# Turning and projecting finished attention tiles inside the last two groups, and a new order of the first context loads

## The reference

```python
q = query @ Wq.T + bq;  k = key @ Wk.T + bk;  v = value @ Wv.T + bv
attn = softmax(q @ k.T)          # layer 0: scaled, masked, then a product with Wo
out = attn @ v
x = x + out
```

## Time and profile before

| what | value |
|---|---|
| median of 3 runs | 1501.59 us (1499.8 to 1501.68) |
| the profiled execution | 1503.77 us, its span 1502.0 us |
| PE busy | 1430.5 us, 95% of the span |
| DVE, ACT, POOL busy | 64%, 50%, 22% |
| mean granted clock of PE | 0.987 of full speed |
| stage 0 with its start; stages 3 and 6 | about 0 to 151 us; 363 to 491 us; 585 to 715 us |

### The profile page before, as it was taken

How to read it: one execution, slowest core, us unless ns; L and a number is a source line. 1 busy time by engine, 2 the same in 40 slices (tenths; PEclk the granted TensorE clock), 3 DMA queues, 4 the chain that set the end, 5 groups by cost and what they waited for, 6 DMA issues and landing times.

```text
span 1502.0 us, 26221 instructions
## 1 busy us (share of the span) xinstructions
PE 1430.5 (95%) x10513; PEld 979.6 (65%) x10513; DVE 967.1 (64%) x1667; ACT 750.2 (50%) x1379; POOL 331.2 (22%) x439
## 2 busy tenths in 40 slices
PE   7899999999999999999999989999989899999998
PEld 4797666887888655898565545555545454555697
DVE  4776645544787534787363378889989892567533
ACT  5574342113665424664442337777777676325232
POOL 3784340002643213642103041110000000100000
PEclk9999999999999999999999999999999999999999
DMA  9314132221212410211315365545757412310140
GB/s 373 129 57 181 63 121 92 95 85 36 73 69 107 151 59 35 91 57 55 106 70 186 51 173 92 85 76 87 177 79 146 93 20 106 161 57 2 57 169 14
DMA packets 43008, 147.74 MB, mean 98 GB/s; under 512 B 6380, under 2 KB 21996, under 8 KB 34028
## 3 DMA queue, kind: packets, MB, share of 16 engines
q1 hardware_dynamic: 42888, 146.07, 33.7%
HBM read 123.49 MB, written 22.56 MB: 97 GB/s over the span
## 4 chain that ended last, share of the span: by engine, by line
PE 83%; DVE 9%; ACT 4%; issue 2%; POOL 2%; DMA 0%; SPq 0%; ACTq 0%; POOLq 0%; DVEq 0%
PE PS L163 51%; PE PS L2399 8%; PE PS L2311 7%; PE PS L2296 5%; PE PS L634 2%; PE PS L1660 2%; DVE SM L2415 2%; PE PS L1889 1%; POOL CNr L932 1%; PE PS L1910 1%; PE PS L2390 1%; PE PS L2985 1%; PE PS L1917 1%; PE PS L2890 1%; DVE SM L306 1%
## 5 line engine op out<-in xcount | busy, mean ns | idle before, releaser
L2415 DVE TENSOR_REDUCE SM<-PS 128x1 f32<-128x1024 f32 x256 | 301.8, 1219 | 42.4 <-PE PS L2296 41.1
L163 PE MATMUL PS<-ARr 128*128 128x256 f32 (+1 forms) x672 | 177.2, 323 | 0.8 <-POOL CNr L932 0.8
L2311 PE MATMUL PS<-AR 49*128 49x256 bf16 (+1 forms) x1216 | 162.9, 271 | 1.1 <-DVE AR L2436 0.7
L163 PE MATMUL PS<-HT,AR 128*128 128x512 f32 x328 | 153.4, 616 | 2.6 <-ACT HT L355 1.1
L163 PE MATMUL PS<-CNr,ARr 128*128 128x256 f32 x672 | 130.7, 292 | 11.6 <-DVE ARr L801 10.7
L2311 PE MATMUL PS<-AR,CT 49*128 49x256 bf16 (+1 forms) x832 | 124.6, 272 | 0.0
L163 PE MATMUL PS<-ARr,HTr 128*128 128x512 f32 x384 | 122.3, 400 | 0.5 <-issue 0.5
L163 PEld LDWEIGHTS PS<-ARr 128*128 128x128 f32 x672 | 114.9, 190 | 10.1 <-issue 1.2
L862 ACT CAST ARr<-PS 128x512 fp32r<-128x512 f32 x96 | 56.3, 586 | 112.5 <-PE PS L634 112.5
L163 PEld LDWEIGHTS PS<-HT,AR 128*128 128x128 f32 x328 | 61.4, 195 | 78.0 <-issue 74.1
L163 PE MATMUL PS<-AR 128*128 128x256 f32 (+3 forms) x504 | 109.5, 371 | 1.4 <-DVE AR L720 0.8
(11 more groups left out here) (403 smaller groups left out, 2727.7 us busy)
## 6 DMA issues: line engine op xcount, KB each, us to landing
CN<-ctx_n SPq DMA_DIRECT2D x24, 1024.0 KB, 5.6
AR<-k_parts SPq DMA_DIRECT2D x114, 128.0 KB
k_parts<-CN SPq DMA_DIRECT2D x32, 384.0 KB, 3.3
CT<-pack SPq DMA_DIRECT2D x6, 2048.0 KB, 7.6
AR<-pack SPq DMA_DIRECT2D x20, 512.0 KB, 4.6
CT<-k_parts SPq DMA_DIRECT2D x78, 128.0 KB
CT<-ctx_t SPq DMA_DIRECT2D x8, 1024.0 KB, 19.1
v_ones<-CN SPq DMA_DIRECT2D x28, 288.0 KB, 3.0
```

Of the source, the lines that this page charges most:

```text
L163: last = te.matmul(o, l, r, start=first and k == 0, stop=final and k == n - 1, skip_group_check=True)
L2311: return te.matmul(PS[:, b, z * 256:z * 256 + 256], keys[rows, c * 128:c * 128 + 128], QQ9[rows, pr, rest, cols], start=not rest, stop=boo ...
L2415: ve.tensor_reduce(MX9[:, p % 2, e, g % 8 // 4, g % 4:g % 4 + 1], PS[:, b:b + 2, :].rearrange("p a b -> p (a b)"), AX, ALU.max).then_inc(* ...
```

## The change

In stages 3 and 6 the first two tiles are turned and projected inside groups 14 and 15; in stage 0 they are turned there. Products of all three stages take their banks from a ring of their own, YR. The first four pieces of the two context forms are asked for alternately.

```diff
+        YR = banks.ring((0,), (1,), (4,), (5,))
...
                 def product(i, src, Wf, *points):
-                    b, before = PB.take(("y", s, i), ("x", s, i))
+                    b, before = YR.take(("y", s, i), ("x", s, i))
...
                     if g < 14:
                         score(g + 2, 1)
+                    if g == 14:
+                        turn_mixed(0)
+                        turn_mixed(1)
                     if g < 15:
                         turn(g + 1, 0)
-                    else:
-                        turn_mixed(0)
-                        turn_mixed(1)
                     mix(g, 1)
+                    if g == 14 and not project:
+                        product(0, OT, Wv, ("ot", s, 0))
+                    if g == 15 and not project:
+                        product(1, OT, Wv, ("ot", s, 1))
                 turn_mixed(2)
...
                 else:
-                    product(0, OT, Wv, ("ot", s, 0))
-                    product(1, OT, Wv, ("ot", s, 1))
                     turn_mixed(3)
                     product(2, OT, Wv, ("ot", s, 2))
                     product(3, OT, Wv, ("ot", s, 3))
...
                     sums(g + 1)
+                    if g == 14:
+                        turn_mixed(0)
                 add_mixed(14)
                 rest_of_weights(15, 1)
-                turn_mixed(0)
                 add_mixed(15)
...
+                turn_mixed(1)
                 head_of_weights(15, 1)
-                turn_mixed(1)
                 turn_mixed(3)
...
-        def load_context(sp, s, b):
-
-            for q in range(4):
+        def load_context(sp, s, b, quarters=range(4)):
+
+            for q in quarters:
...
                 for q in range(4 * b, 4 * b + 4):
                     se.dma_start(CT[:, :, q * 1024:q * 1024 + 1024], ctx_t[:, :, q * 1024:q * 1024 + 1024]).then_inc(
                         *sp.lands(f"ct{q}", "ct", q))
-                if b == 0:
-                    load_context(sp, 0, 0)
+                    if b == 0:
+                        load_context(sp, 0, 0, [q])
```

## The result

The changed kernel takes 1499.19 us (median of 22 runs), the one before on the same chips 1502.85 (22 runs): ratio 0.9975, interval 0.9963 to 0.9986. A gain of 0.8 was forecast, so 2.9 us were missing.

What follows compares the result with a forecast made beforehand. PE carries 83% of the chain, but at the edited ends it waits for ACT and DVE. Terms 0 - 0.2 + 1.7 - 0.3 - 2.0 = -0.8 us, from the median 1501.6 to 1500.8; range 1497.4 to 1503.6.

Steps and rivals of the forecast that it cites:

- Loads: 0: First context loads in stage 0: the new order gains nothing, since no read but the first waited for a transfer.
- Stage 0's end: -0.2: Turning tiles 0 and 1 in the 0.90 us hole before turn(15,0) lets mix(15,1) begin 0.2 us earlier.
- Stage 3's end: +1.7: Waits added on PE's queue and for bank 5 move the whole tail 1.7 us later; bounds +0.8 to +3.4.
- the additions behind the copy of tile 2: Stage 3's end: DVE's additions to X queue behind its copy of tile 2, so the first begins 0.8 us later.
- the bank-5 wait: Stage 4's first job takes product(3)'s bank 5 and waits for the fourth addition; PE idles 1.7 us.
- the first rival: Clock stays up in stages 3 and 6: stage 3 costs 0.8, stage 6 gains 3.0, sum -2.7, 1498.9 us; chance 0.20.
- The rule that the prediction cited: Transposes do not count as busy for PE's clock gate; then the clock-stays-up rival falls and the sum stays -0.8 us.
- Stage 6's start: -0.3: First score no longer waits 0.51 us for ACT's copy out of bank 1; worth 0.25 to 0.5 us.
- Stage 6's end: -2.0: Tail without its two bank waits: product(2) begins at 711.46, not 713.47, gaining 2.0 us; bounds 1.3 to 3.0.
- the clock's stretches move: One of three signs, in the new profile, by which the prediction would call itself wrong; no size given.
- The long stall: Rival: stage 0's 9.25 us DVE operation gets in after a single POOL operation, gaining 8.9 us, 1491.9; chance 0.05.

Runs made afterwards that it cites:

- kernel 1: Only the order of the first context loads changed, against the kernel before: 1503.97 us, ratio 1.0002.
- 3: The changed kernel with the old order of the first context loads: 1500.63 us, ratio 0.9992 to the kernel before.
- kernel 6: Changed kernel with product banks 0, 5, 1, 4, and tile 2 turned ahead of product(1) in stages 3 and 6: 1494.24 us, ratio 0.9947 to before.
- 2: Only the products' own ring of four banks added, against the kernel before; turns and products stay in place: 1500.63 us, ratio 0.998.
- 4: Changed kernel with the products' banks in the order 0, 5, 1, 4, giving bank 5 to product(1): 1496.92 us, ratio 0.9961 to before.
- kernel 7: Kernel 4 plus ten unread products in bank 7, behind a wait for DVE's addition of group 13, before turn(15,0): 1503.72 us, ratio 1.0007 to before.
- 11: Kernel 2 with tiles 0 and 1 turned in the hole before turn(15,0), all products at the tail: 1495.93 us, ratio 0.9943 to before.
- 12: Kernel 11 with product banks 0, 5, 1, 4, POOL's wait in stage 0 and eight unread products in a free bank: 1484.94 us, ratio 0.9882 to before.
- 8: Kernel before with only the common bank ring moved on within stage 6, 4 places at its start, 2 at its end: 1497.36 us, ratio 0.9971.
- kernel 5: Kernel 4 plus one POOL wait in stage 0 until DVE has taken group 2's running sum: 1488.76 us, ratio 0.9912 to before.
- kernel 10: Kernel 9 plus eight unread products in a free bank ahead of the turns of tiles 0 and 1: 1483.97 us, ratio 0.9865 to before.
- kernel 9: Kernel 6 plus POOL's one wait in stage 0: 1488.08 us, ratio 0.9875 to before.

## Why the prediction was right, and where it was not

**Loads: 0.** Right (kernels 1 and 3). In the changed kernel's trace `ct` 1 was issued at 4.15 and landed 14.3 us later, at 18.5 (19.1 by the forecast), and ACT read it at 22.94.

**Stage 0's end: -0.2.** The step gave 0.26 (26.37 to 26.11). What it missed is a fall of the clock that the one trace of before did not show. With the turns at the tail it fell in three of four traces (27.94, 27.92, 27.95 against 26.37, so 1.6 us each time); with them in the hole, and nothing waiting there, in none of nine that I read. By these counts the step is worth 27.55 - 26.1 = 1.4 us in the mean, an estimate from four traces and nine.

**Stage 3's end: +1.7.** Both of its mechanisms were right: the additions behind the copy of tile 2 (kernel 6) and the bank-5 wait (kernels 2 and 4). It was worked out with the clock at half, and that was wrong. The clock stayed up, as the first rival had it, with 0.63 us of waiting for DVE's copy in its place. In the pair of traces the stage lost 1.30, and that rival's +0.8 was too low, since it hid the bank wait. Counted from the last reduction, mix(15,1) began 0.26 earlier than before (0.4 later was forecast), the first addition 0.34 later (0.8), and the first job waited 1.33 (1.7).

Over all the traces, the clock fell here in four of four kernels with the turns at the tail, in none of nine with the turns in the hole, and once more in kernel 7, where PE waited in the hole for 1.98 us. Kernels 11 and 12, with product(0) at the tail, kept the clock too, so it is the turns in the hole, not product(0), that go with it. At stage 6's end the same edit did not hold the clock: it fell in three of four traces with the turns at the tail (before, 1, 8) and in four of nine with them in the hole (changed, 5, 6, 11), which tells little either way.

The rule that the prediction cited ("TensorE: Matmul & The Clock Gate" of the Trainium skill, Part 4: PE-mode transpose, where transposes do not count as busy) spoke against this rival; here the four transposes, 0.43 us of work, went with a clock that stayed up. The counts do not tell whether it is their work or the shorter idle time behind them.

**Stage 6's start: -0.3.** 203.30 to 202.93 for the stretch, 0.37, with the fall at 596.7 gone. The wait of 0.51 ended at 596.42, ahead of that fall, and so was not at half clock, as the step had it. PE's idle time also moved. Timeline of PE, first the kernel before, then the changed one:

```profile
604.49 0.66 PE L634 MATMUL PS<-CST,AR 128*128 128x128 f32 x4 [0.68 <-ACT AR L871]
607.76 1.68 PE L163 MATMUL PS<-CNr,ARr 128*128 128x256 f32 x12 [0.78 <-DVE ARr L801]
```

```profile
602.46 0.63 PE L635 MATMUL PS<-CST,AR 128*128 128x128 f32 x4 [1.13 <-ACT AR L875]
606.86 1.65 PE L163 MATMUL PS<-CNr,ARr 128*128 128x256 f32 x12 [1.92 <-POOL CNr L936]
```

PE comes sooner to its first turn and first mix and waits longer there, 1.92 us for POOL's rest of the context. In traces 5, 6, 10 and 11 the clock fell behind this wait, 26 to 27 us after the stage's first turn (14.8 in the trace of before), and the stretch was 204.1. So the edit took away one fall and left room for another, 12 us further on.

**Stage 6's end: -2.0.** -1.45 in the pair. The missing half microsecond has two parts. PE began what stands behind mix(15,1) 12.44 us after the last reduction, where it was 11.76 before: 0.68 later, not 0.38. And from there to product(2) it took 1.76 where the step had 1.59, with 0.30 of waiting for DVE's copy of tile 2. Kernel 6, which turns tile 2 ahead of product(1), takes 0.52 off this end.

**The sum.** -0.8 was forecast, and the pair's stretches give -0.26 + 1.30 - 0.37 - 1.45 = -0.8, but this agreement holds for that pair alone, and in it stage 3 (0.4 less than forecast) and stage 6's end (0.55 short) cancel: that is luck. The spans of the pair differ by 2.8. The other 2.0 lie outside the stretches: 1.2 ahead of stage 0's last reduction, where the trace of before has the clock at half for 6.8 us from 9.6 on and the changed one has not, and 0.8 from stage 7 on. Such an early fall stands in the traces of before, 1, 4, 5, 7 and 12 and in none of the other eight, with either order of the loads.

The prediction called itself wrong if the clock's stretches move, and by that sign it was: they moved at the end of stage 3 and the start of stage 6. Its time held, its account of the clock did not. The term that was mis-sized is stage 0's, and with it the mean over executions: the prediction took the clock of one trace as given. With the means of the like traces (before and 1; changed and 3; for stage 0 all four with the turns at the tail) it is -1.4 + 1.3 - 0.3 - 1.8 = -2.2 us, inside the interval of 2.1 to 5.6. The clock says the same from another side: over 224 runs, within one kernel, 0.001 less of mean clock went with 1.1 us more, and the change raised it from 0.9878 (88 runs) to 0.9920 (22 runs). Where the falls beyond these places went stays open. Some of them are in stage 9, whose code the change did not touch (last section).

**The long stall** stayed, as 0.95 of the chances had it. That rival's price for it, 8.9 us, came true in kernel 5: 7.4 to 8.2 by the runs, 9.0 by the stretches. Its way did not: DVE was to get in at the end of a single POOL operation, but in kernel 5 it missed one such change and got in when POOL rested.

## What to carry to other kernels

Move work into a hole only if nothing in it waits. Four transposes whose input had long been there cost nothing and, at the ends of stages 0 and 3, went with a clock that stayed up, while products that depended on a copy on another engine, or a filler that depended on a bank, held up the engine's queue for 2 us a stage. When a ring of banks is split, work out which later work takes the bank of the last reader: one place in the order was worth 1.6 us. And look first at the longest instruction whose size does not explain its time: one wait on another engine won more than all moves of work together.

## What the runs showed of the hardware

**One DVE operation starved beside POOL, and 55 like it did not.** In the trace of before 56 operations of DVE of this form (`scalar_tensor_tensor` of one column, all in SBUF) overlap POOL's tensor operations up to the end of stage 6. One took 9.25 us and missed thirteen changes from one POOL operation to the next. The other 55 ended with a POOL operation or within 0.1 us of the start of the next, and took at most 0.78 us; at the end of 36 of them POOL went on without a rest. One of the 36, from DVE's timeline and POOL's:

```profile
68.70 0.38 DVE L772 SCALAR_TENSOR_TENSOR SM<-SM 128x1 f32<-128x1 f32 x1
```

```profile
68.33 2.84 POOL L932 TENSOR_TENSOR CNr<-CN,ARr 128x256 fp32r<-128x256 f32 x4
```

The long one stands at the same place in all ten traces without POOL's wait (9.21 to 9.26 us). 0.09 us of rest ended it in kernel 5, but a rest is not what the others needed. Why this one missed the changes is open.

**PE stopped by itself in stage 9.** In the midst of a series of products PE stood still for 1.4 to 2.9 us with nothing to wait for ("issue"), and in some cases the clock fell behind it. From kernel 9, first the timeline, then stretches of 1 us:

```profile
1058.48 0.40 PE L2404 MATMUL PS<-AR,CN 128*32 128x256 f32 x1 [2.04 <-issue]
```

```profile
1059.00:1060.00 1.00, 1.00 (x13) 0.62 (x10) 0.00 (x0) 0.00 (x0) 0.00 (x0) 0.77 1.06 394
1060.00:1061.00 1.00, 1.00 (x14) 0.50 (x13) 0.91 (x1) 0.64 (x2) 0.00 (x0) 0.50 1.06 392
```

There were four such stops between 880 and 1260 us in the traces of before and of kernels 1, 6, 8 and 11, two in the changed kernel and 2, 3, 4, 5 and 9, one in 7 and 12, none in 10. From stage 7's first turn to the end the code and its banks are the same, and it took 774.4 us (kernel 10) to 783.3 (kernel 1), 781.8 before and 781.0 changed. That is a spread of 9 us for the same code, as large as most of the scatter between runs of one kernel (12 us for the 22 runs of before). What causes the stops, and whether their number depends on the kernel, was not settled.
